# Experts of a mixture layer: from every expert on every row to rows sorted by expert in DRAM

## What is computed

```
x = x + _L0_ffn_ref(_layernorm(x))            # b*s = 4096 rows, h = 256
shared_out = (silu(x @ shared_gate) * (x @ shared_up)) @ shared_down      # width 256
router_probs = softmax(x @ router)                                        # 8 experts
topk_probs, topk_idx = top_k(router_probs, 2)
coef = sum(one_hot(topk_idx, 8) * topk_probs[..., None], axis=2)          # 6 of 8 are zero
expert_out[e] = (silu(x @ gate[e]) * (x @ up[e])) @ down[e]               # width 128 each
out = sum_e(expert_out[e] * coef[:, e]) + shared_out
x = x + _L1_xattn_ref(_layernorm(x), ...)     # the second attention
```

## Time and profile before

| | us |
|---|---|
| median of 3 runs | 1131.69 |
| lowest and highest | 1131.4, 1134.55 |
| the profiled execution, its own time | 1133.72 |
| its span, first to last instruction | 1132.0 |

### The profile page before, as it was taken

The page is one execution under the profiler, slowest core; times in us unless marked ns, Lnnn a source line. Parts: engine busy times, 40 slices in busy tenths (PEclk is TensorE's granted clock), DMA queues, the critical chain, the costliest instruction groups (busy, mean ns, idle before and its releaser), DMA issues. The chain is left out here.

```text
span 1132.0 us, 24944 instructions
## 1 busy us (share of the span) xinstructions
PE 990.9 (88%) x9211; PEld 783.0 (69%) x9226; DVE 823.7 (73%) x1997; ACT 583.2 (52%) x1094; POOL 492.0 (43%) x493
## 2 busy tenths in 40 slices
PE   5798999995699999999999967999999957888886
PEld 4577777773588888888888855777777734544444
DVE  3688887775757667767666564777777738988896
ACT  2466566664433333233332335666666527777775
POOL 2344444442132322323223313444444438999991
PEclk9799999998799999999999987999999969999998
DMA  7700000000000000000000040000000000000000
GB/s 217 189 2 2 2 2 2 2 2 2 1 1 1 0 0 0 0 0 0 0 0 0 1 144 2 2 2 2 2 3 2 2 1 10 24 24 19 25 24 29
DMA packets 19421, 20.98 MB, mean 19 GB/s; under 512 B 6528, under 2 KB 17920, under 8 KB 19072
## 3 DMA queue, kind: packets, MB, share of 16 engines
q1 hardware_dynamic: 17712, 19.12, 5.4%
q10 hardware_dynamic: 1616, 0.58, 0.3%
HBM read 15.51 MB, written 4.19 MB: 17 GB/s over the span
## 5 line engine op out<-in xcount | busy, mean ns | idle before, releaser
L432 POOL TENSOR_TENSOR sm_a<-sm_a,mx_a 128x616 f32<-128x616 f32 x128 | 155.8, 1218 | 257.2 <-DVE mx_a L604 257.2
L743 POOL TENSOR_TENSOR hl_f<-hf_f,hh_f 128x512 fp32r<-128x512 f32 x80 | 103.5, 1294 | 261.5 <-ACT hh_f L867 261.5
L862 ACT ACTIVATE sg_f<-pGU_f 128x512 f32<-128x512 f32 x80 | 47.9, 599 | 169.0 <-PE pGU_f L768 169.0
L597 DVE TENSOR_TENSOR sm_a<-pS_a,mask 128x616 f32<-128x616 f32 x128 | 101.1, 792 | 38.2 <-PE pS_a L474 38.2
L766 PE MATMUL pGU_f<-xh_f,wgh_f 128*128 (+1 forms) x320 | 128.3, 401 | 0.0
L767 PE MATMUL pGU_f<-xl_f,wgh_f 128*128 (+1 forms) x320 | 125.1, 391 | 0.0
L768 PE MATMUL pGU_f<-xh_f,wgl_f 128*128 (+1 forms) x320 | 124.8, 390 | 0.0
L973 DVE TENSOR_TENSOR hf_f<-pGU_f,sg_f 128x512 f32<-128x512 f32 x80 | 55.4, 692 | 91.6 <-ACT sg_f L862 91.6
L983 DVE SCALAR_TENSOR_TENSOR x<-pD_f,coef_f,x 128x256 f32 (+1 forms) x256 | 106.2, 477 | 17.2 <-PE pD_f L805 15.7
L554 ACT ACTIVATE pr_a<-sm_a 128x616 f32<-128x616 f32 x128 | 91.5, 715 | 49.0 <-POOL sm_a L432 49.0
L503 PE MATMUL pO_a<-pt_a,V 128*32 128x128 f32 x2048 | 104.4, 276 | 2.1 <-DVE x L629 2.1
(11 more groups left out here) (196 smaller groups left out, 2250.3 us busy)
## 6 DMA issues: line engine op xcount, KB each, us to landing
x<-x_in SPq DMA_DIRECT2D x4, 1024.0 KB, 13.5
out_x<-x SPq DMA_DIRECT2D x32, 128.0 KB, 1.7
gu<-gu_in SPq DMA_DIRECT2D x1, 2560.0 KB, 9.6
aw<-aw_in SPq DMA_DIRECT2D x2, 1024.0 KB, 11.1
w<-w_in SPq DMA_DIRECT2D x2, 1024.0 KB, 6.3
dn<-dn_in SPq DMA_DIRECT2D x1, 1280.0 KB, 12.0
b<-b_in SPq DMA_DIRECT2D x1, 512.0 KB, 8.9
g<-g_in SPq DMA_DIRECT2D x1, 512.0 KB, 9.7
```

The lines of the kernel that those rows point to most:

```text
L432: pool.tensor_tensor(heads, heads, mx[u][:, g, :].rearrange("p (h a) -> p h a", a=1).broadcast_to([P, HG, SK]), ALU.subtract).then_inc(shi ...
L597: dve.tensor_tensor(sm[u][:, g, :].rearrange("p (b h k) -> p b h k", b=2, k=SK), pS[:, 2 * g:2 * g + 2, 0:HS].rearrange("p b (h k) -> p b ...
L743: pool.tensor_tensor(hl[u][:], hf[u][:], f32(hh[u][:]), ALU.subtract).then_inc(hl_ok, 1)
```

## The change

The weights come in 15 pieces of 512 columns of both matrices through four buffers, and they are split while the first attention runs: in steps 8 to 22 ACT rounds a piece (`round_weights`) and POOL takes the rest (`residue`). SP first writes 9.7 MB of zeros over a DRAM tensor `slots` of 72 x 128 rows with 264 values (256 of x, 8 coefficients).

The mixture has three parts now. First all 32 tiles are normalised, half by DVE and half by POOL, turned, and multiplied by the router in f32. One chain of some 30 DVE instructions over all tiles finds the two best experts of every row and the row's place in the list of each, where an expert's list begins at a multiple of 128 rows. Second, PE runs the shared expert for all rows (16 units as before; the low rest is DVE's now) while POOL scatters every tile twice into `slots` with an indirect DMA, 64 in all, at most 8 in flight. Third, the 72 slots of 128 rows are worked off as 36 pairs, each slot with the weights of the one expert that owns it: PE and DVE read the owner of a slot from a table into registers, 8 slots at a time. SP loads a pair into one of 4 buffers and stores its result to the DRAM tensor `mixed`.

The second attention gets the results by 64 indirect DMAs of POOL, each of which gathers 128 rows of `mixed` and adds them to a tile of x: 28 of them in the keys stage, the rest in the steps of the attention. Since x is complete only then, the second attention takes its statistics in its own steps, as the first does.

```diff
+def fetch(pool, dram, sb, t, a):
+    if a > 0:
+        pool.wait_ge(sb["got"][a - 1][t % 4], 16 * (t // 4 + 1))
+    if t >= 4:
+        pool.wait_ge(sb["got"][a][t % 4], 16 * (t // 4))
+    pool.indirect_dma_start(sb["x"][:, t, :], None, dram["mixed"][:],
+                            bass.IndirectOffsetOnAxis(sb["idx"][a][:, t:t + 1], 0),
+                            compute_op=ALU.add).then_inc(sb["got"][a][t % 4], 16)
...
 keys_phase, POOL, layer 1:
-            keys_of(pool, 1)
+                for n in range(NB):
+                    pool.wait_ge(sb["mixed_in"][n], 16 * (NPAIR // NB))
+                for t in range(4):
+                    fetch(pool, dram, sb, t, 0)
+                for t in range(4):
+                    fetch(pool, dram, sb, t, 1)
+                    fetch(pool, dram, sb, t + 4, 0)
+                keys_of(pool, 1)
+                for t in range(4, FETCHED):
+                    fetch(pool, dram, sb, t, 1)
+                    fetch(pool, dram, sb, t + 4, 0)
...
 attention_phase, POOL:
             def step(t, u, has):
                 if has(1):
                     shift(t + 1, 1 - u, 0)
                     shift(t + 1, 1 - u, 1)
                     bias(t + 1)
+                if layer == 1:
+                    gather(t)
+                if layer == 0 and 0 <= t - SPLIT_FROM < PIECES:
+                    residue(t - SPLIT_FROM)
...
 moe_phase, SP:
+            def load(i):
+                if i >= NB:
+                    sp.wait_ge(s_mixed, i - NB + 1)
+                sp.dma_start(sx[i % NB][:], slot_rows(dram["slots"], i)).then_inc(loaded[i % NB], 16)
+            def store(i):
+                sp.wait_ge(s_out, i + 1)
+                sp.dma_start(slot_rows(dram["mixed"], i),
+                             ys[i % NB].rearrange("p (j d) -> p j d", j=2)).then_inc(sb["mixed_in"][i % NB], 16)
+            for n in range(MOVES):
+                sp.wait_ge(moved[n], 16 * (TOPK * T // MOVES))
+            for i in range(NB):
+                load(i)
+            for i in range(NPAIR):
+                if i + NB < NPAIR:
+                    load(i + NB)
+                store(i)
...
 moe_phase, POOL:
+            for t in range(1, T, 2):
+                pool.tensor_scalar(rows[:, t, 0:D], X[:, t, :], sb["rs"][:, t:t + 1], sb["nm"][:, t:t + 1],
+                                   ALU.mult, ALU.add).then_inc(normed_p, 1)
...
+            for a in range(TOPK):
+                pool.wait_ge(placed, a + 1)
+                for t in range(T):
+                    n = a * T + t
+                    if n >= MOVES:
+                        pool.wait_ge(moved[n % MOVES], 16 * (n // MOVES))
+                    pool.indirect_dma_start(dram["slots"][:], bass.IndirectOffsetOnAxis(idx[a][:, t:t + 1], 0),
+                                            rows[:, t, :], None).then_inc(moved[n % MOVES], 16)
...
 moe_phase, PE, one pair of slots (slot_gate_up, slot_down) and the order of the pairs:
+                for j in range(2):
+                    e = at_of[2 * i + j]
+                    out = bG[u][:, j * D:(j + 1) * D]
+                    for k in range(G):
+                        high, low = wgh[:, k, bass.ds(e, D)], wgl[:, k, bass.ds(e, D)]
+                        pe.matmul(out, pair_part(xh, u, j, k), high, start=(j == 0 and k == 0), stop=False, skip_group_check=True)
+                        pe.matmul(out, pair_part(xl, u, j, k), high, start=False, stop=False, skip_group_check=True)
+                        mm = pe.matmul(out, pair_part(xh, u, j, k), low, start=False, stop=(k == G - 1),
+                                       skip_group_check=True)
...
+            for i in range(-2, NPAIR + 1):
+                if i + 1 >= 0 and (i + 1) % 4 == 0 and i + 1 < NPAIR:
+                    owners((i + 1) // 4)
+                if i + 2 < NPAIR:
+                    slot_turn(i + 2, i % 2)
+                if 0 <= i + 1 < NPAIR:
+                    slot_gate_up(i + 1, (i + 1) % 2)
+                if 0 <= i < NPAIR:
+                    slot_back(i, i % 2)
+                if i >= 1:
+                    slot_down(i - 1, (i - 1) % 2)
```

More of the change, by code:

```diff
@@ L649, in step @@
             def step(t, u, has):
-                if layer == 0 and ahead(t)[-1] < T:
+                if ahead(t)[-1] < T:
                     early_stats(t)
@@ new lines, in moe_phase @@
+        turned = sbt("turned", [P, 4 * D])
+        xt = [turned[:, i * D:(i + 1) * D] for i in range(4)]
+        desc, n128 = sbt("desc", [P, NE]), sbt("n128", [P, NSLOT])
+        wide = lambda n: sbt(n, [P, T, NE])
+        first, second, every, work, ex = wide("first"), wide("second"), wide("every"), wide("work"), wide("ex")
+        best, key, total = sbt("best", [P, T]), sbt("key", [P, T]), sbt("total", [P, T])
+        upto, before = sbt("upto", [P, NE, T]), sbt("before", [P, NE, T])
+        room, ends, bases = (sbt(n, [P, NE]) for n in ("room", "ends", "bases"))
@@ new lines, in _ @@
+        @block.sync
+        def _(sp):
+            def load(i):
[14 more added lines that the diff above has]
+                store(i)
@@ new lines, in _ @@
+            dve.tensor_tensor(work[:], work[:], ranked, ALU.mult).then_inc(chain, 1)
+            dve.wait_ge(chain, 3)
+            dve.tensor_reduce(key[:], work[:], AX.X, ALU.max).then_inc(chain, 1)
+            dve.wait_ge(chain, 4)
+            dve.tensor_tensor(first[:], work[:], per_tile(key[:]), ALU.is_equal).then_inc(chain, 1)
+            dve.wait_ge(chain, 5)
+            dve.scalar_tensor_tensor(every[:], first[:], -HUGE, logits, ALU.mult, ALU.add).then_inc(chain, 1)
+            dve.wait_ge(chain, 6)
@@ new lines, in _, with x_low @@
+            dve.wait_ge(chain, 11)
+            dve.tensor_tensor(every[:], first[:], second[:], ALU.add).then_inc(sel_ok, 1)
+            def x_low(g, j):
+                dve.wait_ge(xh_ok, ST * g + j + 1)
+                for k in range(G):
+                    last = dve.tensor_tensor(xpart(xl, g, k, j * P, P), x_bank(g, j)[:, k * P:(k + 1) * P],
+                                             f32(xpart(xh, g, k, j * P, P)), ALU.subtract)
+                last.then_inc(xl_ok, 1)
+            for j in range(ST):
+                x_low(0, j)
@@ new lines, in _ @@
+            dve.tensor_scalar(room[:], room[:], MAGIC, None, ALU.add).then_inc(chain, 1)
+            dve.wait_ge(chain, 17)
+            dve.tensor_tensor(before[:], before[:], by_expert(within), ALU.add).then_inc(placed2, 1)
+            dve.wait_ge(chain, 18)
+            dve.tensor_scalar(room[:], room[:], -MAGIC, float(P), ALU.add, ALU.mult).then_inc(chain, 1)
+            dve.wait_ge(chain, 19)
+            dve.tensor_tensor_scan(ends[:], sb["ones"][:, 0:NE], room[:], 0.0, ALU.mult, ALU.add).then_inc(chain, 1)
@@ new lines, in _ @@
+            dve.tensor_tensor(second[:], second[:], place, ALU.mult).then_inc(chain, 1)
+            dve.wait_ge(chain, 23)
+            dve.tensor_reduce(best[:], first[:], AX.X, ALU.add).then_inc(chain, 1)
+            dve.wait_ge(chain, 24)
+            dve.tensor_reduce(key[:], second[:], AX.X, ALU.add).then_inc(chain, 1)
+            dve.wait_ge(chain, 25)
+            dve.tensor_copy(idx[0][:], best[:]).then_inc(placed, 1)
+            dve.wait_ge(chain, 26)
+            dve.tensor_copy(idx[1][:], key[:]).then_inc(placed, 1)
@@ new lines, in _, with owners @@
+            for n in range(-1, NCH):
+                if n >= 0:
+                    product(n, n % 2)
+                if n >= 2 and n % 2 == 0:
+                    add(n // 2 - 1)
+                if n >= 0:
+                    low(n, n % 2)
+                for g, j in turns_at(n):
+                    x_low(g, j)
+                if n == 0:
+                    table()
+            add(NG - 1)
+            column = {}
+            def owners(q):
+                _, found = nc.values_load_multi_w_load_instructions(
+                    tab_c[0:1, q * 8:(q + 1) * 8], engines=[mybir.EngineType.DVE])
+                for n, v in enumerate(found):
+                    column[q * 8 + n] = v
```

781 lines of the change are left out of this document (454 added, 327 removed).

## The result

| | before | after |
|---|---|---|
| median of 4 runs, us | 1132.26 | 1185.49 |
| lowest and highest | 1131.4, 1134.55 | 1182.79, 1190.53 |
| ratio after/before, 95% interval | | 1.047 [1.044, 1.050] |
| span of the profiled execution | 1132.0 | 1184.9 |

A forecast was written before the change was run, and what follows sets the result against it. PE's matmuls were taken to bound the mixture (379.9 us). Mixture -106, second keys +13, second attention +14, first attention +6 gave -73 us: 1060.7 from the profiled 1133.7, forecast 1059 as median; range 1008 to 1130.

The forecast's parts named there:

- Part 2, scatter: Mixture: 64 indirect DMAs on POOL at 1.3 us each, 83 us plus 2 of landing, ending at 121 us.
- A: Rival: an indirect DMA costs POOL about 1.0 us or less, so the scatter hides; total about 1035; chance 0.24.
- B: Rival: an indirect DMA costs POOL 2.2 us, total 1166, slower than before; break-even at 1.9 us; chance 0.11.
- Part 2, "beside it": Mixture: shared expert on PE, 66 us plus some 7 of turns, runs beside the scatter and ends near 110 us.
- Part 1, routing: Start of the mixture: normalising by DVE and POOL takes 17 us, logits at 20.5 us, rows' places known at 36.
- Part 3, pairs of slots: Mixture: 36 rounds of 4.0 us, 144 plus 6 for filling and draining; PE 2.8 us a pair, loads landing in 3.6.
- C: Rival: slots bound by PE's sequencer handling registers, a round of 4.8 us or more, total 1088; chance 0.21.
- Parts 4 and 5, gathers: Second keys: 28 gathers at 1.3 us, plus 13 us; second attention: two gathers a step just hidden, some 2 us lost, 3 ahead.
- Part 5, early statistics: Second attention: early statistics return at 0.29 us a step over 31 steps, 9 us.
- Part 6: First attention: ACT's rounding delays 15 steps by 0.4 us, plus 6 us; writing the zeros needs 47 us.
- D: Rival: the zeros hold up the first pieces of weights, total 1084; chance 0.06.

The follow-up runs named there:

- e18: Changed kernel with one short POOL MEMSET of 8 columns behind each of the 64 scattering indirect DMAs: 1131.7 us, ratio to before 0.9974.
- e1: Changed kernel with POOL's scatter waiting until the shared expert is done: 1200.4 us.
- e7: Changed kernel without its 64 gathers, their semaphores raised at once, so the experts' results are left out of x: 1132.8 us.
- e14: Changed kernel with shared-expert units in loops on ACT and DVE alone, PE keeping straight-line code and the right tiles: 1131.7 us, ratio to before 0.9992.
- e16: Changed kernel with two POOL additions of 128x256 behind each scattering indirect DMA: 1218.9 us.
- e9: Changed kernel, straight-line code, with PE's turns of groups 2 to 7 all taking tiles 8 to 11: 1190.4 us.
- e11: Changed kernel with the scatter's indices counting up, row n of the moves to row n of the slots: 1187.4 us.
- e12: Changed kernel with all 64 scattering indirect DMAs taking their rows from tile 0: 1190.9 us.
- e5: As e2, but each turn takes its own tile, which ACT first copies to a fixed buffer: 1199.2 us.
- e6: As e5, plus one unused matmul of 512 columns behind each of the 32 routing turns: 1191.3 us.
- e10: As e5, but ACT copies tiles 8 to 11 over and over: 1197.0 us.
- e2: Changed kernel with shared-expert units 1 to 12 of 16 in loops on PE, ACT and DVE, PE turning tiles 8 to 11 each time: 1134.9 us.
- e13: As e2, but each turn takes its own tile from a fixed buffer filled by SyncE's DMAs, without copies by ACT: 1136.1 us.
- e15: Changed kernel with shared-expert loops on PE alone, turns from tiles 8 to 11 over and over: 1133.4 us.
- the best version: e14 plus one unused matmul of 512 columns behind each of the 32 routing turns: 1129.8 us, ratio to before 0.9953.

## Why the prediction was wrong, point by point

- **Part 2, scatter: right.** Its price was 1.3 us each, measured 1.27; 64 lasted from 333.3 to 414.5, 81.2 us against 83 forecast. At most 8 in flight never held POOL for more than 0.3 us. So A (1.0 us) and B (2.2 us) were both off for the scatter.
- **Part 2, "beside it": the step that failed.** I took it that the scatter and the shared expert run beside each other at no cost to TensorE: I summed PE's 66 + 7 us and POOL's 83 as if each ran alone, and took the longer. The only contention that I had weighed was DVE's. e18 does what the forecast assumed: its mixture lasts 304.3 us in place of 362.6, and this 58 us is more than the whole loss of 53. What the runs showed in its place is PE at one matmul per 2.5 to 2.8 us while indirect DMAs follow each other directly, 118 matmuls in 82 us. No row of before could have shown it, since before has no indirect DMA; a bound for the overlap itself, from nothing hidden to all hidden, was missing from the range. Wholly in turn, as in e1, is 74 us more (110 + 85 in place of 121), and on top of the upper end of 1130 it would have held the result.
- **Part 1, routing: mis-sized.** Logits came 40.5 us after the start, not 20.5. I had DVE's and POOL's normalising as the limit, shut out by each other. They did 16 tiles each in 8.9 and 9.2 us, side by side. (That the 1.60 us of the earlier trace rows come behind a POOL operation of another kind was a misreading: the 0.55 at 925.15 has one before it too, at 924.44.) The limit was PE: turns and an 8-column product in f32, 1.17 us a tile, 37.6 us for 32, of which my sum had only the last tile's 1 us. The clock stood at 0.50 in the opening of the earlier trace rows already, which the prediction doesn't use, and here it stayed at 0.50 with PE 96% busy. The chain behind it took 16 us as forecast, so places were known at 56 against 36: +20.
- **Part 3, pairs of slots: the time right, in part by luck.** 158 us against 153. The middle round took 4.2 us, and 3.9 where PE waited for no load; I had given PE 2.8 and left the rest to the loads. The matmuls with addresses from registers are dearer than the 0.117 of the earlier trace rows: 12 took 2.24 us, 6 took 0.99. C's mechanism was there at little more than half its size, and the loads held PE up less than my 3.6 us of landing made of it (2.9 in e18, whose trace has them). In my own sum the two errors cancel: (3.9 + 1.3 + 2.9) / 2 = 4.05. The timeline of after shows a turn that waits for its load, the first matmuls behind it, and the next turn, which doesn't wait:

```profile
539.78 0.66 PE L1014 MATMUL pL_f<-ident,sx_f 128*128 128x128 f32 x4 [0.73 <-DMA sx_f<-slots]
540.27 0.38 PE L1026 MATMUL pGU_f<-wgh,xh_f 128*128 x1
540.50 0.27 PE L1027 MATMUL pGU_f<-wgh,xl_f 128*128 x1
540.61 0.31 PE L1028 MATMUL pGU_f<-wgl,xh_f 128*128 x1
...
543.72 0.60 PE L1014 MATMUL pX_f<-ident,sx_f 128*128 128x128 f32 x4
```

- **Parts 4 and 5, gathers: mis-sized.** I gave the gather, which adds, the price of the scatter, which doesn't. The group of after's gathers, and then its timeline: a subtraction, two gathers and the second subtraction of a step, and the first of the next step.

```profile
L182 POOL DMA_INDIRECT x<-mixed,idx x64 | 102.6, 1603 | 245.5 <-DMA mixed<-turned_f 226.8 <-issue 14.7 <-DMA x<-mixed,idx 2.1
```

```profile
739.21 1.22 POOL L511 TENSOR_TENSOR sm_a<-sm_a,mx_a 128x616 f32<-128x616 f32 x1 [1.86 <-DVE mx_a L708]
...
741.27 1.56 POOL L182 DMA_INDIRECT x<-mixed,idx  x1
743.13 1.55 POOL L182 DMA_INDIRECT x<-mixed,idx  x1 [0.30 <-issue]
744.12 1.81 POOL L511 TENSOR_TENSOR sm_a<-sm_a,mx_a 128x616 f32<-128x616 f32 x1
...
747.79 1.22 POOL L511 TENSOR_TENSOR sm_a<-sm_a,mx_a 128x616 f32<-128x616 f32 x1 [1.86 <-DVE mx_a L708]
```

1.60 us busy and 0.26 of idle time on the mean: 1.86 each. Two are 3.7 us where the earlier trace rows leave 2.7, the subtraction behind them takes 1.81 in place of 1.22, and a step lasts 8.6 us in place of 6.9, in some 12 steps: 20 us. That is rival B's mechanism, at its break-even of 1.9, but only for the gathers. In the keys 28 of them took 59 us from 641.3 to 700.1, and nothing there could hide them; forecast 36. At 1.86 each they are 52; the rest is POOL's own operation, one wait of 2.05 us for an earlier gather to land, and three gathers of 2.2 to 3.2 us. The stage then ends 3.7 us after the last one, where I had 2.5 for landing and operation together. The semaphores of PE's matmuls come on time in both stages, so the slowdown isn't there.
- **Part 5, early statistics: right,** 8.8 us (e7) against 9. **Part 6: 0 instead of +6;** the zeros landed in 39 us (I had 47), and rounding and rests found their gaps. D didn't occur.
- **The Trainium skill,** page "SBUF — State Buffer", section "SBUF: two separate sides", has DVE and GpSimd under a lock that also keeps GpSimd from writing descriptors; the case that it describes is a DVE operation in a two-port mode. In this case, with DVE at its full work (e14, e18), the 64 indirect DMAs were busy for 65.2 us, and with DVE idle (e1) for 61.7; single ones took 1.38 to 1.46 in place of 0.96. Beside DVE's work they take 3.5 us more in all, and no run shows that this lock is the reason.

With the keys (+26 on the forecast), the attention (+17), the routing (+20) and the slowdown (+58) the forecast of 1059 becomes 1180. The rest: from the last indirect DMA to the first turn of a slot it takes 6 us (e18), of which I had counted 2, the slots took 5 more, and Part 6 gives 6 back: 1183. The lower end of the range doesn't follow from its own terms, since 1035 less 22 is 1013 and not 1008; for the result it makes no difference.

**What stays open.** Why back-to-back indirect DMAs of GpSimd slow TensorE is not settled. Shown is when: never beside plain DMAs, never with another POOL instruction between two of them (e16, e18), always, without such an instruction, with straight-line code on all three engines (after, e7, e9, e11, e12), always with ACT's copies in the loops (e5, e6, e10), never with loops and no such copies (e2, e13, e14, e15). Each arrangement is one kernel, so this is a list of cases and not a rule. The slowdown begins 4 to 8 us after the first indirect DMA and outlasts the last by 8 to 9, and the times of one kernel lie close together (1182.8 to 1190.5 for after). What loops and copies have to do with it I can't say. The runs with loops also count some semaphores from one and address tiles otherwise; straight-line code on all three engines in that form wasn't run, so the loops themselves aren't shown to be what spares e2, e13, e14 and e15. Whether a MEMSET between two gathers would make these cheaper wasn't tried, nor e18 with the fillers.

## What to carry to other kernels

An overlap of two engines that share no operand is a forecast of its own, to be given bounds like a price; where the profile has an engine issuing matmuls that wait for nothing at a fraction of their pace, look at the moments at which their semaphores change, and at what runs beside them. A chain of indirect DMAs on GpSimd beside a busy TensorE should be measured with a short instruction between them. And sorting rows by expert brought PE's part of the experts from 265 us (64 units of 4.14) to 146 (its busy time in the pairs of slots) here, but moving the rows twice by index (64 x 1.27 + 64 x 1.86 = 200 us of POOL) left a gain of 0.5% in the best version, where other work covers most of the scatter and part of the gathers.

## What the runs showed that I had not expected

- TensorE at one matmul per 2.5 to 2.8 us beside back-to-back indirect DMAs (118 matmuls in 82 us), and none of it with a MEMSET of 0.12 us between them (423 in 84), at the same 1.27 us from one to the next.
- A TensorE busy for 38.3 of 40 us with turns of 128 columns and products of 8 was granted 0.50 of its clock throughout; with one matmul of 512 columns more for each tile it was granted 0.90, and the 32 tiles were through 7 us earlier.
- An indirect DMA of 128 rows: 1.27 us from start to start when it scatters rows of 1056 bytes, 1.86 when it gathers rows of 1024 bytes and adds. A plain DMA of the same rows on GpSimd: 0.54.
